# Causal masks moved from matmuls to GpSimd selects, and FFN weight loads, splits and the end of attention put in another order

## What is computed

```python
h = _layernorm(x) * (1 + ca) + sa
x = x + ga * attention(h)
h = _layernorm(x) * (1 + cb) + sb
x = x + gb * ffn(h)
```

```python
mask = pos[None, :] < pos[:, None]
scores = jnp.where(mask, einsum('bhtd,bsd->bhts', q, k) * scale, NEG_BIG)
attn = softmax(scores) * row_valid
out = einsum('bhts,bsd->bhtd', attn, v) @ Wo.T + bo
```

## Time and profile before

| | |
|---|---|
| median of 3 runs | 671.88 us |
| lowest, highest | 670.19, 679.08 us |
| the profiled execution's own time | 665.51 us |
| its span in the trace | 663.7 us |
| PE, PEld busy | 606.6, 471.5 us |
| DVE, ACT, POOL busy | 379.0, 302.3, 129.3 us |
| mean granted clock of PE | 0.984 |

### The profile page before, as it was taken

The page is one execution under the profiler, slowest core; times in us unless marked ns, Lnnn a source line. Parts: engine busy times, 40 slices in busy tenths (PEclk is TensorE's granted clock), DMA queues, the critical chain, the costliest instruction groups (busy, mean ns, idle before and its releaser), DMA issues.

```text
span 663.7 us, 10873 instructions
## 1 busy us (share of the span) xinstructions
PE 606.6 (91%) x3897; PEld 471.5 (71%) x3907; DVE 379.0 (57%) x757; ACT 302.3 (46%) x462; POOL 129.3 (19%) x137
## 2 busy tenths in 40 slices
PE   3898899798999999999998897889997999999995
PEld 3777645487788888888886565543445878888884
DVE  6477535966244444544457699792358543345455
ACT  3657275554233333333333473427864643333331
POOL 4501015323122222222230000000112331222220
PEclk9999899999899999999999899898999999999999
DMA  8364454100001111111100024301210001111101
GB/s 324 98 223 173 145 162 153 50 1 25 24 26 48 47 47 47 47 47 47 47 25 0 1 69 133 121 5 62 81 56 25 1 25 47 48 47 47 43 7 63
DMA packets 22194, 44.64 MB, mean 67 GB/s; under 512 B 3632, under 2 KB 7632, under 8 KB 22160
## 3 DMA queue, kind: packets, MB, share of 16 engines
q1 hardware_dynamic: 21840, 44.05, 20.8%
q10 hardware_dynamic: 320, 0.13, 0.1%
HBM read 33.16 MB, written 11.01 MB: 67 GB/s over the span
## 4 chain that ended last, share of the span: by engine, by line
PE 67%; DVE 19%; ACT 4%; issue 4%; DMA 2%; POOL 2%; SPq 0%; DVEq 0%; ACTq 0%; POOLq 0%
PE PS L557 32%; PE PS L980 16%; DVE nmx L1531 5%; PE PS L857 3%; PE PS L827 2%; PE PS L701 2%; PE PS L703 2%; DVE x L1601 1%; PE PS L601 1%; DMA w_raw<-in_wqkv 1%; PE PS L714 1%; DVE stats L1430 1%; DVE xn L1743 1%; ACT q_masked L1129 1%; PE PS L872 1%
## 5 line engine op out<-in xcount | busy, mean ns | idle before, releaser
L1273 ACT ACTIVATE qk_hi<-xn 128x512 fp32r<-128x512 f32 x82 | 51.7, 631 | 171.0 <-DVE xn L1743 139.6
L557 PE MATMUL PS<-h_hi,wqkv_hi 128*128 128x512 f32 x304 | 102.7, 395 | 1.9 <-DVE h_lo L1464 1.3
L557 PE MATMUL PS<-h_hi,wqkv_lo 128*128 128x512 f32 x272 | 92.8, 396 | 2.6 <-DVE xn L1653 2.6
L1740 DVE TENSOR_TENSOR prs<-prs,PS 128x512 f32<-128x512 f32 x60 | 41.2, 687 | 86.8 <-PE PS L557 78.3
L1747 DVE TENSOR_TENSOR qk_lo<-xn,qk_hi 128x512 fp32r<-128x512 f32 x70 | 48.4, 692 | 47.8 <-ACT qk_hi L1273 47.8
L1269 ACT ACTIVATE prs<-PS 128x512 f32<-128x512 f32 x82 | 48.7, 594 | 48.5 <-PE PS L557 48.5
L557 PEld LDWEIGHTS PS<-h_hi,wqkv_hi 128*128 128x128 f32 x304 | 57.2, 188 | 14.0 <-DVE h_lo L1464 1.7
L557 PE MATMUL PS<-h_lo,wqkv_hi 128*128 128x512 f32 x160 | 62.9, 393 | 0.0
L557 PEld LDWEIGHTS PS<-h_hi,wqkv_lo 128*128 128x128 f32 x272 | 51.1, 188 | 14.9 <-DVE xn L1653 4.3
L1531 DVE TENSOR_REDUCE nmx<-PS 128x512 f32 (+4 forms) x96 | 54.2, 637 | 4.4 <-PE PS L719 4.3
L980 PE MATMUL PS<-wqkv_hi,qk_hi 128*128 128x256 f32 x288 | 53.5, 285 | 0.9 <-POOL qk_lo L529 0.7
(11 more groups left out here) (251 smaller groups left out, 1223.4 us busy)
## 6 DMA issues: line engine op xcount, KB each, us to landing
fw_raw<-in_ffn SPq DMA_DIRECT2D x41, 384.0 KB, 3.1
qk_slot<-rows_scr SPq DMA_DIRECT2D x32, 200.0 KB
rows_scr<-qk_hi SPq DMA_DIRECT2D x16, 256.0 KB
qk_slot<-q_scr SPq DMA_DIRECT2D x32, 100.0 KB
rows_scr<-qk_lo SPq DMA_DIRECT2D x8, 256.0 KB
wmod<-in_wmod SPq DMA_DIRECT2D x1, 1536.0 KB, 14.3
x<-in_x SPq DMA_DIRECT2D x2, 512.0 KB, 4.0
wmod<-in_wmod SPq DMA_DIRECT2D x1, 1024.0 KB, 10.8
```

The costliest lines, as they stand in the source:

```text
L557: ins = nc.tensor.matmul(dst, left(a, c), right(b, c), start=n == 0, stop=n == total - 1)
L1273: nc.scalar.activation(hidR[b][0], hid[b], ACT.Copy).then_inc(f["hi"], 1)
L1740: tt(hid[buf] if half is None else gu[buf], gact[buf], PS[:, 5, :], ALU.mult).then_inc(f["gu"], 1)
```

## The change

1. In the second layer's attention pass the mask matmuls are gone. After each exponential GpSimd sets the probabilities on and above the diagonal to zero with `affine_select` (`clear_above`, one select for thirds 0 and 2, two for third 1, each over both heads of the pair, 128 x 256), and raises `sel`. `values` waits for `sel`, block by block, in place of `p`. Query 0 keeps its own key so that its sum isn't zero (its output is set to zero as before); the mask table of the maxima pass has the same exception.
2. The loads of FFN tiles 2 and 3 move to behind heads 13 and 19 in both passes. GpSimd's splits of tiles 0, 1 and 2 stand at the head of quads 2, 3 and 4, ahead of that quad's values or selects and of its `out_low`. ScalarE's high half of tile 2 moves to behind exponential 4n-1.
3. At the start, an exponential of one element (`exp_table`) stands before the last `max_high` of each layer, and in the first layer `gates` moves to behind the second exponential, PE's wait for it to the first `values`.
4. At the end of a pass DVE normalises before `outputs(BQ + 1)` and makes `h_low` before `outputs(BQ + 3)`. PE's projection of the last chunk of batch 1 (`out_projection_rest`) stands behind `early_up(0)`.

```diff
--- before.py
+++ after.py
@@ -97,8 +97,8 @@
         maskB = sb("maskB", [P, 5 * KEYS0 + 3 * P], BF16)
         mask0 = [maskB[:, 0:2 * KEYS0], maskB[:, KEYS0:3 * KEYS0]]
         mask0T = maskB[:, 3 * KEYS0:5 * KEYS0]
-        mask1 = maskB[:, 5 * KEYS0:5 * KEYS0 + 2 * P]
-        mask1T = maskB[:, 5 * KEYS0 + 2 * P:]
+        mask1 = maskB[:, 5 * KEYS0:5 * KEYS0 + P]
+        mask1_first = maskB[:, 5 * KEYS0 + P:]
         headmask = sb("headmask", [P, H])
         zeroR = sb("zeroR", [P, P], F32R)
         zeroB = sb("zeroB", [P, P], BF16)
@@ -260,7 +260,7 @@
         for l in range(2):
             at.append({n: sem(f"at{l}_{n}") for n in (
                 "qk0", "qk1", "qk2", "qk3", "qm", "s", "mxd", "mt", "mhi", "mlo", "mw0", "mw1", "st", "p", "vs", "o", "oe",
-                "rd", "on", "od", "oz", "oh", "ol")})
+                "rd", "on", "od", "oz", "oh", "ol", "sel")})
         ff = []
         for l in range(2):
             ff.append({n: sem(f"ff{l}_{n}") for n in (
@@ -392,8 +392,8 @@
                     sp.wait_ge(at[l][f"mw{b}"], 16 * 2)
                     for u in range(b * H, (b + 1) * H):
                         load_keys_major(l, u)
-                        if u in (H + 5, H + 10):
-                            s = (u - H) // 10
+                        if u in (H - 3, H + 3):
+                            s = u // H
                             load_ffn(l, 1, s, 2 + s)

             sp.wait_ge(consts, CONSTS)
@@ -501,14 +501,30 @@
                 if l == 0:
                     pool.wait_ge(v_taken, 2 * B)
                     take_values(0)
+                else:
+                    for j in range(PER_QUAD[1]):
+                        clear_above(j)
                 for g in range(QUADS):
+                    if g in (2, 3, 4):
+                        weights_low(l, g - 2, g % 2)
                     if l == 0 and g + 1 < QUADS:
                         take_values(g + 1)
+                    elif l and g + 1 < QUADS:
+                        for j in range(PER_QUAD[1] * (g + 1), PER_QUAD[1] * (g + 2)):
+                            clear_above(j)
                     if g % 2:
                         out_low(l, g // 2)
-                    if g in (2, 3, QUADS - 2):
-                        i = min(g - 2, 2)
-                        weights_low(l, i, i % 2)
+
+            def clear_above(j):
+
+                third, p = j % THIRDS, j // THIRDS
+                pool.wait_ge(at[1]["p"], j + 1)
+                tile = pair1[p % SLOTS]
+                for kb in ((0,), (1, 3), (2,))[third]:
+                    part = tile[:, :, START1[kb]:START1[kb] + P]
+                    pattern, base, step = ([[0, 2], [P - 1, P]], 1, -P) if kb == 0 else ([[0, 2], [1, P]], 0, -1)
+                    ins = nc.gpsimd.affine_select(part, part, pattern, ALU.is_gt, 0.0, base, step)
+                ins.then_inc(at[1]["sel"], 1)

             def weights_low(l, i, s):

@@ -717,7 +733,7 @@
                 def masked(qt):
                     bank, col = BANK1[qt]
                     return nc.tensor.matmul(PS[:, first + bank, col + qt * P:col + WIDTH1[qt]], identB[:, :],
-                                            mask1[:, 0:WIDTH1[qt] - qt * P], start=False, stop=True, skip_group_check=True)
+                                            mask1 if qt else mask1_first, start=False, stop=True, skip_group_check=True)

                 products(0)
                 products(1)
@@ -824,17 +840,9 @@
                     col = START1[kb] % S
                     for h in range(2):
                         rows = slice(HALF * h, HALF * h + ROWSP)
-                        nc.tensor.matmul(PS[:, 2 * third + h, col:col + n], k1[rows, b, kb * P:(kb + 1) * P],
-                                         qk[s][rows, kb * P:S], start=i == 0, stop=True, skip_group_check=i > 0,
-                                         tile_position=(HALF * h, 0))
-                for h in range(2):
-                    if third == 1:
-                        both = PS[:, 2 * third + h, :].rearrange("p (k q) -> p k q", q=P)[:, 0:NT:NT - 1, :]
-                        ins = nc.tensor.matmul(both, identB[:, :], mask1T.unsqueeze(1).to_broadcast([P, 2, P]),
-                                               start=False, stop=True, skip_group_check=True)
-                    else:
-                        ins = nc.tensor.matmul(PS[:, 2 * third + h, 0:P], identB[:, :], mask1T, start=False, stop=True,
-                                               skip_group_check=True)
+                        ins = nc.tensor.matmul(PS[:, 2 * third + h, col:col + n], k1[rows, b, kb * P:(kb + 1) * P],
+                                               qk[s][rows, kb * P:S], start=i == 0, stop=True, skip_group_check=i > 0,
+                                               tile_position=(HALF * h, 0))
                 ins.then_inc(a["st"], 1)

             def values(l, g, blocks):
@@ -843,9 +851,13 @@
                 if blocks[0] == 0:
                     ge(a["oe"], g - (1, 0)[l])
                     if l == 0:
+                        if g == 0:
+                            pe.wait_ge(gate_taken, 2)
                         pe.wait_ge(a["vs"], SLOTS * (g + 1))
-                    pe.wait_ge(a["p"], PER_QUAD[l] * (g + 1))
+                        pe.wait_ge(a["p"], PER_QUAD[l] * (g + 1))
                 for kb in blocks:
+                    if l:
+                        pe.wait_ge(a["sel"], PER_QUAD[1] * g + THIRDS + (1, 2, 3, 2)[kb])
                     for s in range(SLOTS):
                         slot = SLOTS * (g % 2) + s
                         if l == 0:
@@ -884,8 +896,6 @@
                 for s in range(2):
                     keys_major(l, s)
                 pe.wait_ge(at[l]["mlo"], B)
-                if l == 0:
-                    pe.wait_ge(gate_taken, 2)
                 n = PER_QUAD[l]
                 for j in range(2, n):
                     keys_major(l, j)
@@ -926,6 +936,8 @@
                 zero(Y1_BANK, Y1_BANK + 1)
                 pe.wait_ge(at[l]["ol"], CHUNKS - 1)
                 project_out(l, 1, range(OC - 1), False)
+
+            def out_projection_rest(l):
                 pe.wait_ge(at[l]["ol"], CHUNKS)
                 project_out(l, 1, range(OC - 1, OC), False)

@@ -1014,6 +1026,7 @@

                 pe.wait_ge(hl_ready, 4 * n + 2)
                 early_up(0)
+                out_projection_rest(l)
                 early_up(1)
                 logits(l, 0)
                 zero(0, 1)
@@ -1140,6 +1153,9 @@
                     for s in range(SLOTS):
                         mask_q(l, b, g, s)

+            def exp_table():
+                nc.scalar.activation(table_in[:, :], ct[:, 0, 0, 0:1], ACT.Exp)
+
             def max_high(l, b):

                 a = at[l]
@@ -1184,6 +1200,7 @@
             take_v(1)
             max_high(0, 0)
             mask_rest(0, 1)
+            exp_table()
             max_high(0, 1)

             def exponentials1(j):
@@ -1208,7 +1225,6 @@
                     return
             def attention(l):
                 if l == 0:
-                    gates(0)
                     act.wait_ge(split, 3)
                 n = PER_QUAD[l]
                 for u in range(n * QUADS):
@@ -1216,8 +1232,10 @@
                         exponentials1(u)
                     else:
                         exponentials(l, u)
-                    if u in (2 * n - 1, 3 * n - 1, 7 * n - 2):
-                        i = u // n - 1 if u < 4 * n else 2
+                    if l == 0 and u == 1:
+                        gates(0)
+                    if u in (2 * n - 1, 3 * n - 1, 4 * n - 1):
+                        i = u // n - 1
                         weights_high(l, i // 2, i % 2)

             def take_rows(l):
@@ -1627,11 +1646,11 @@
                 aggregate = gate_and_add(l, 0, 0, 1, Y0_BANK[l][1])
                 aggregate()
                 norm_scales(n, slice(0, 1))
+                normalise(n)
                 outputs(l, BQ + 1)
-                normalise(n)
                 outputs(l, BQ + 2)
+                h_low(n, 0)
                 outputs(l, BQ + 3)
-                h_low(n, 0)
                 dve.wait_ge(y_ps, 4 * l + 3)
                 first = gate_and_add(l, 0, 1, 0, Y1_BANK)
                 dve.wait_ge(y_ps, 4 * l + 4)
@@ -1849,7 +1868,9 @@
     causal = np.where(np.arange(P)[None, :] < q, 0.0, NEG)

     bandT = np.where((c >= q) & (c <= q + WIN), 0.0, NEG)
-    mask = np.concatenate([first, later, bandT, causal, np.full((P, P), NEG), causal.T], 1).astype(np.float32)
+    own = causal.copy()
+    own[0, 0] = 0.0
+    mask = np.concatenate([first, later, bandT, causal, own, np.full((P, P), NEG)], 1).astype(np.float32)
     headmask = (q // DH == np.arange(H)[None, :] % (P // DH)).astype(np.float32)
     tri = np.broadcast_to(np.tril(np.ones((16, 16)), -1), (P, 16, 16)).astype(np.float32)

```

## The result

| | before | after |
|---|---|---|
| median on this chip (4 runs each) | 675.02 us | 702.88 us |
| lowest, highest | 670.19, 679.08 | 700.55, 703.83 |
| profiled execution, its span | 665.51, 663.7 | 700.55, 698.8 |
| mean granted clock, profiled execution | 0.984 | 0.941 |

The ratio is 1.0476, with an interval of 1.0432 to 1.0519: slower by 28 us, about twice the 14.8 of the sum.

The account below looks back on a forecast made before the run. PE, busy 91% of the span, was taken as the bound. First attention +8.5, second +3.5 and clock +2.8 gave +14.8 on the unprofiled median of 671.9, so 686.7 us; 8-in-10 range 677 to 694.

Parts of the forecast that it names:

- The block at pair 7 and 10: PE waits for key rows queued behind FFN loads: 9.1 us in first attention, 7.1 and 3.0 (pair 10) in second.
- Masks and start: Masks off PE in second attention: -8.1 us; exponential table loaded early and gates later in first attention: -0.9 us.
- The end of each pass: DVE normalising before outputs(5) delays the last values and projection: +0.7 us in first attention, +1.5 in second.
- The clock: Low clock after the 9 and 7 us PE stalls, 1.4 us each: +2.8 us, bounds 0 and 5.
- Dear selects: Rival: a GpSimd select takes 0.74 us, so GpSimd falls behind; +21 us, 693 us; chance 0.15.
- Clock kept: Rival: stalls as worked out, no low clock, second block absorbed; +9.6 us, 681.5 us; chance 0.20.
- The block doesn't bite: Rival: pair 7's keys arrive in time and both stalls vanish; -7 us, 665 us; chance 0.12.
- The larger gain from the end order: Rival: no stalls at pair 7, and each pass's end gains 3 us or more; under 659 us; chance 0.03.

Follow-up runs that it names:

- fillers: The changed kernel with zero matmuls (38, 31 and 16) ahead of PE's three waits for late key rows; 695.45 us, ratio 1.035.
- edit1_alone: The kernel before with only the GpSimd selects in place of the mask matmuls; 671.41 us, ratio 1.002.
- edit1_warm: The kernel before with the selects, plus two zero matmuls ahead of each of pieces 3 to 7 of the second attention; 666.30 us, ratio 0.994.
- split_first: The changed kernel with GpSimd's splits of FFN tiles 0 and 1 one quad earlier, loads left alone; 679.97 us, ratio 1.013.
- end_alone: The kernel before with only the new order at the end of each pass; 685.30 us, ratio 1.017.
- edit1_zeros: The kernel before with the selects, its mask matmuls kept but adding zeros; 682.10 us, ratio 0.999.
- before_warm: The kernel before with eight zero matmuls in PE's idle time at the start of the first attention; 666.18 us, ratio 0.989.
- best: The kernel before with the selects, the new start, and zero matmuls at the start of both attentions (4 and 10); 662.04 us, ratio 0.982.
- start_alone: The kernel before with only the early exponential table and the later gates; 669.44 us, ratio 0.987.
- edit2_back: The changed kernel with the moves of FFN loads and splits undone; 672.39 us, ratio 1.002.
- loads17: The changed kernel with the first FFN load behind head 17 instead of 13; 687.26 us, ratio 1.020.

## Why the prediction was right in direction and wrong in size

- **The block at pair 7 and 10: right.** 9.21, 7.15 and 1.54 us for 9.1, 7.1 and 3.0. The last was forecast too long although its keys came later than worked out, 11.3 us behind the resumption (496.41 to 507.70) for 10.2. PE wanted them later still, after 9.75 for 7.2, for its clock was 0.50 up to 503.4; so here too it was the clock that the working lacked.
- **Masks and start: right.** -7.7 at equal clock for -8.1; from the first piece of the first pass to its fifth 4.40 us for 5.43, so 1.0 gained for 0.9.
- **The end of each pass: right in its chain, if anything too dear in its price.** +0.5 at equal clock for 0.7 + 1.5. outputs(5) did start behind the normalisations, 6.76 us behind DVE's first step after the projection for 4.90 before (1.9 later for 1.7), and values(6) did wait (3.73 us), but the projection's waits for the low half went in exchange, and the sum had no term for that.
- **The clock: the step that failed.** The sum had "+2.8", two low stretches of 1.4. What it should have been: over its runs the mean clock of after is 0.934, that of before 0.966. About 11 us of low clock in after lie on an idle PE (103.9 to 108.7, 493.0 to 496.4, 523.7 to 526.2), worth 0.5 x 11 / 700 = 0.008 of the mean and no time. The rest is (0.032 - 0.008) x 585 = 14 us, five times the term. Added to a change without clock of 7.8 + 0.008 x 585 = 12.5 us (12.0 forecast; 13.4 in fillers) it makes the 26.5 us that lie between the means. Against the 32 runs of before up to 676 us (clock 0.975, mean 670.5) it is 19 us, seven times the term, and again 12.6 are left without it.

The term was small for two reasons that can be told apart. The price of one stretch came from the 3.4 us one at 451 to 454 of the earlier trace rows, while the stretches at and behind the stalls lasted 7 to 10 us. And their number came from counting stalls: two. After had six more stretches than before in its profile, some of them ahead of any stall (83 to 93, which stands, some us shifted, also in edit1_alone and edit1_warm, which don't have edit 2), so not each of them is due to the edit of the loads. What that edit does to the clock is 0.966 to 0.941 alone, and 0.962 to 0.934 in company: 0.025 and 0.028, some 15 us, less the idle part. The upper bound of 5 us for the term was as wrong as the term, and with it the range. With 14 in the place of 2.8 the forecast is 697.9, and 701.0 from the 675.0 that before had on this chip, against 702.9.

There was a second flaw, in what the sum stood on. The profiled execution of before had a clock of 0.984, which none of its 51 runs here exceeds. A trace from the best run shows the short stretches only; that before itself loses up to 32 us to the clock in other runs could not be read from it, though 665.5 against a median of 671.9 was a hint: at 5.9 us for 0.01 those 6.4 us are a clock of 0.973.

The Trainium skill, page "TensorE: Matmul & The Clock Gate", section "HAM oscillation — how this bites in real kernels", puts the price of waiting for a DMA between bursts of matmuls at half of the throttled time. The trace agrees in kind: low clock follows the stalls, and filling the first one left 1.00 behind it. By that rule, applied to the low time over a busy PE, my estimate for the profiled pair is (82 - 11 - 20) x 0.5 = 25 us, where the line gives (0.043 - 0.008) x 585 = 20. Half would be the price if PE were the bound in all of it; that in part of it it isn't is my reading, and no run tests it.

The rival to set beside mine would have been one with a larger clock term: 14 to 20 us of the loss are clock, and the stalls and the rest some 12.5.

**The rivals.** Dear selects: fell, 0.408 us. Clock kept: fell, the clock was half of the loss or more. The block doesn't bite: fell in after, and split_first shows what it asks for, the split released one quad earlier. The larger gain from the end order: fell, end_alone is not faster.

**What stays open.** Why one low stretch lasts 3.4 us and another 10 with the same instructions, and why the same kernel meets them in some runs only. Whether the data of the matmuls matters to the clock: edit1_zeros was to say, and with eleven runs in two clusters it doesn't. Whether split_first with edit 4 undone would keep edit 2 harmless: not run.

## What to carry to other kernels

An in-order queue that carries both prefetches and the loads of the running loop must not get a wait whose release hangs on the loop's own later work; compare when the release comes with when the first load behind it is wanted, as here to 0.1 us for the first two stalls. Where PE is the bound, price a stall of PE twice, once for its length and once for the clock around it, and take the second from the clock over many runs of the kernel rather than from its best profile. Idle time of PE that can't be removed can be filled: in a stall of 9 us zero matmuls left a clock of 1.00 behind it where it had been 0.54. At the start of a pass a few of them left before within 5 us in five runs, where it had spread over 32 in 51, which makes the help likely and doesn't prove it.

## What the runs showed of the hardware

- Granted clock against time: 5.9 us for 0.01 of the mean, residual 1.3 us over 51 runs of one kernel, 0.933 to 0.984.
- Clock at 0.50 for 10 us at a time with PE recorded busy 9.85 of 10 (83 to 93 in after), behind 0.8 us of idle time in the 3 us before. With idle time filled ahead of it, the same place stood at 1.00 (84 to 94 in before_warm and best, PE busy 10.00), but so it did in the profiled runs of before, start_alone, edit2_back, fillers, split_first and loads17, which have no filling there.
- An `affine_select` on GpSimd of 128 x 256 f32 in place: 0.408 us in the median, 1.39 for the first. It costs what a one-input copy does, position test and all.
- A key row that is queued behind an FFN load lands 5.4 us after the split that released that load (103.24 to 108.66), as 5.26 in before; in the second attention, with half the bytes a head, 4.2 (492.16 to 496.40).
